# Two Silu paths of a fused Mamba and mixture kernel: tanh and a DVE product replaced by ACT's Silu

## What is computed

```
x_in = in_proj_w @ ctx;  xc = causal conv over 4 taps
u    = silu(xc + conv_b)                          # 512 channels x 512 steps
dt, B, C = x_proj_w @ u                           # the small projection, 16 + 16 + 16 rows
delta = softplus(dt_proj_w @ dt + dt_b);  A = -exp(A_log)
state[n] = state[n] * exp(delta * A[n]) + delta * u * B[n]      # scan over time, n = 0..15
y = sum_n state[n] * C[n] + D * u
x = x + tanh(g0) * y * silu(layernorm(x))         # z is layernorm(x), laid out channel by time
x = x + tanh(g1) * experts(layernorm(x))          # top 2 of 32, rank 16
```

## Time and profile before

| | us |
|---|---|
| median of 3 runs | 539.43 (539.42 to 541.25) |
| the profiled execution | 541.24 |
| its span | 539.4 |
| PE busy | 489.4 (91%) |
| DVE busy | 476.8 (88%) |
| POOL busy | 454.4 (84%) |
| ACT busy | 398.6 (74%) |

### The profile page before, as it was taken

The page is one execution under the profiler, slowest core; times in us unless marked ns, Lnnn a source line. Parts: engine busy times, 40 slices in busy tenths (PEclk is TensorE's granted clock), DMA queues, the critical chain, the costliest instruction groups (busy, mean ns, idle before and its releaser), DMA issues.

```text
span 539.4 us, 9244 instructions
## 1 busy us (share of the span) xinstructions
PE 489.4 (91%) x3018; PEld 367.8 (68%) x3018; DVE 476.8 (88%) x880; ACT 398.6 (74%) x726; POOL 454.4 (84%) x335
## 2 busy tenths in 40 slices
PE   9989798979677999999989999999899999899687
PEld 5569597758475776668677776667566666676654
DVE  3799999879899999789999999888988989999851
ACT  4698869386867777587968777577888898888542
POOL 1299999959999999979999999989799898987810
PEclk9979999999998999999998999999999999999799
...
DMA packets 18705, 39.36 MB, mean 73 GB/s; under 512 B 5586, under 2 KB 6354, under 8 KB 18659
## 3 DMA queue, kind: packets, MB, share of 16 engines
...
...
## 4 chain that ended last, share of the span: by engine, by line
PE 54%; DVE 19%; ACT 18%; issue 8%; DVEq 0%; POOL 0%; ACTq 0%; POOLq 0%
PE p_s L748 12%; PE p_y L770 11%; DVE state L1262 9%; PE p_v L803 8%; PE p_f L794 6%; ACT da L1007 4%; PE p_tr L717 4%; PE p_pr L692 2%; PE p_pr L680 2%; DVE p_s L1262 2%; ACT p_s L1007 2%; DVE x L1204 2%; ACT pair_b L991 2%; PE p_pr L673 2%; PE p_f L783 2%
## 5 line engine op out<-in xcount | busy, mean ns | idle before, releaser
L573 POOL TENSOR_TENSOR state<-state,c_bc 128x1024 f32<-128x1024 f32 (+1 forms) x131 | 256.7, 1973 | 21.5 <-DVE state L1262 19.2
L748 PEld LDWEIGHTS p_s<-pair_b,du_t 128*128 128x128 f32 x1072 | 139.2, 198 | 44.7 <-issue 31.4
L748 PE MATMUL p_s<-pair_b,du_t 128*128 128x128 f32 x1072 | 153.1, 285 | 16.7 <-DVE state L1262 13.8
L770 PE MATMUL p_y<-ident,state 128*128 128x128 f32 x1024 | 149.5, 276 | 0.0
L558 POOL TENSOR_TENSOR dbu<-du,pair_b 128x1024 f32<-128x1024 f32 (+1 forms) x80 | 145.3, 1818 | 1.7 <-DVE p_s L1262 1.7
L1007 ACT ACTIVATE p_s<-delta,a_neg 128x512 f32<-128x512 f32 (+1 forms) x162 | 93.5, 580 | 65.8 <-DVE state L1280 33.0
L1262 DVE TENSOR_TENSOR_SCAN state<-da,p_s 128x512 f32<-128x512 f32 (+1 forms) x116 | 134.4, 1173 | 6.3 <-PE p_s L748 5.7
L770 PEld LDWEIGHTS p_y<-ident,state 128*128 128x128 f32 x1024 | 121.6, 144 | 23.7 <-issue 22.7
L1007 ACT ACTIVATE da<-delta,a_neg 128x512 f32<-128x512 f32 (+1 forms) x158 | 100.4, 648 | 14.0 <-DVE state L1262 13.7
L1262 DVE TENSOR_TENSOR_SCAN state<-p_s,dbu 128x512 f32<-128x512 f32 (+1 forms) x100 | 98.2, 997 | 1.8 <-POOL dbu L558 1.8
L794 PE MATMUL p_f<-u_sb,h_t 128*128 128x512 f32 x112 | 55.9, 602 | 0.5 <-DVE gw L1365 0.5
...
## 6 DMA issues: line engine op xcount, KB each, us to landing
...
```

Of the source, the lines that this page charges most:

```text
L573: eng.tensor_tensor(pair, pair, c_bc[:, 2 * p:2 * p + 2, c0:c0 + w], ALU.mult).then_inc(po_cs, 1)
L748: mm = eng.matmul(p_s[g % BANKS][:, t * P:(t + 1) * P], du_t[:, f % 2, t, :], diagonals_of(n // 2)[:, n % 2, c0 // P + t, :], start=(t == ...
L770: mm = eng.matmul(p_y[:, t, :], slot(NS * f + n)[:, t * P:(t + 1) * P], ident[:, :], is_transpose=True, start=False, stop=(n == NS - 1 and ...
```

## The change

Both silus are computed by ACT's own function. The conv weights are not halved any more, `tanh_v`, `z_part` and DVE's two products go; `silu_u(q)` and `silu_z(f)` are one ACT instruction each, and the factor tanh(g0) goes into the copy of the turned gate (`copy_sz`). The Silu table is another set than that of Exp and Ln, so the silus are gathered in blocks `silu(f)`: a table load, one or two `silu_z`, none to two `silu_u`, and a load back. Exp and Ln are then both taken from one set, and the two loads around Ln go. The block stands at n = 9 behind decay 9 and the skip term, in phases 1, 3, 7 and 11 at n = 0 behind the first decay. There is a block in each of phases 1 to 12, and in 14, 16 and 18; phase 1 makes the gates of blocks 0 and 1 and u of block 5, phase 2 the gate of block 2 and u of blocks 4 and 6, phase f from 3 to 11 the gate of f and u of f + 4, and phases 12, 14, 16, 18 the gates of two halves. `zh` gets two buffers. The convolution of blocks 5 and up works in place in the ring of `u` and no longer in `vsp`; that ring has five slots in place of six. POOL's six small operations for z become four. PE and SP have the same instructions in the same order as before.

```diff
@@ -17,7 +17,7 @@
 BANKS = 3
-U_RING = 6
+U_RING = 5
...
@@ -134,6 +134,20 @@
+    SILU_Z = {1: [0, 1]}
+    SILU_Z.update({f: [f] for f in range(2, SPLIT)})
+    SILU_Z.update({f: [f, f + 1] for f in range(SPLIT, F, 2)})
+    SILU_U = {1: [5], 2: [4, 6]}
+    SILU_U.update({f: [f + 4] for f in range(3, SPLIT)})
+    def zh_before(f):
+        if f < SPLIT + 2:
+            return f - 2 if f < SPLIT else SPLIT - 2
+        return SPLIT - 1 if f < SPLIT + 4 else f - f % 2 - 3
     HELD = {11: [0, 1], 12: [2, 3], 13: [4, 5], 14: [6], 15: [7]}
...
@@ -188,8 +202,8 @@
         zv = sb("zv", [P, 2, Q])
-        zr = sb("zr", [P, 2, 4, Q])
-        zh = sb("zh", [P, L])
+        zr = sb("zr", [P, 2, 2, Q])
+        zh = sb("zh", [P, 2, L])
         sz_t = sb("sz_t", [P, Q, P])
...
@@ -356,7 +367,7 @@
-        ZOPS = 6
+        ZOPS = 4
         FOPS = 3
...
@@ -575,18 +585,14 @@
                 if b >= 2:
-                    eng.wait_ge(ac_z, 2 * Q * (b - 1))
+                    eng.wait_ge(ac_z, Q * (b - 1))
                 eng.tensor_tensor(zv[:, 0, :], zmv[:, :, 1], eps_c[:, :], ALU.add).then_inc(po_zs, 1)
                 eng.wait_ge(po_zs, ZOPS * b + 1)
-                eng.tensor_tensor(zv[:, 1, :], zv[:, 0, :], minus_half[:, :], ALU.pow).then_inc(po_zs, 1)
+                eng.tensor_tensor(zr[:, b % 2, 0, :], zv[:, 0, :], minus_half[:, :], ALU.pow).then_inc(po_zs, 1)
                 eng.wait_ge(po_zs, ZOPS * b + 2)
-                eng.tensor_tensor(zr[:, b % 2, 0, :], zv[:, 1, :], half[:, :], ALU.mult).then_inc(po_zs, 1)
-                eng.tensor_tensor(zv[:, 0, :], zv[:, 1, :], minus_half[:, :], ALU.mult).then_inc(po_zs, 1)
-                eng.wait_ge(po_zs, ZOPS * b + 4)
-                eng.tensor_tensor(zr[:, b % 2, 1, :], zmv[:, :, 0], zv[:, 0, :], ALU.mult).then_inc(po_zs, 1)
-                eng.wait_ge(po_zs, ZOPS * b + 5)
-                eng.wait_ge(ac_k, 2)
-                eng.tensor_scalar(zr[:, b % 2, 2:4, :], zr[:, b % 2, 0:2, :], gx[:, :], None, ALU.mult).then_inc(po_zs, 1)
+                eng.tensor_tensor(zv[:, 1, :], zmv[:, :, 0], zr[:, b % 2, 0, :], ALU.mult).then_inc(po_zs, 1)
+                eng.wait_ge(po_zs, ZOPS * b + 3)
+                eng.tensor_tensor(zr[:, b % 2, 1, :], zv[:, 1, :], minus_one[:, :], ALU.mult).then_inc(po_zs, 1)
...
@@ -919,18 +925,15 @@
                 eng.wait_ge(pe_in, q + 1)
-                if q >= 5:
-                    eng.wait_ge(ve_dl, q - 3)
+                if q >= U_RING:
+                    eng.wait_ge(ac_skip, q - U_RING + 1)
+                    wait_for_du(eng, q - U_RING)
                 eng.activation(conv_v(q), conv_bank(q)[:, :], ACT.Identity, bias=cb[:, q % Q:q % Q + 1],
-            def silu_first(q):
+            def silu_u(q):
                 eng.wait_ge(ve_tap, 3 * q + 3)
                 eng.activation(u[:, q % U_RING, :], conv_v(q), ACT.Silu).then_inc(ac_u, 1)
-            def tanh_v(q):
-                eng.wait_ge(ve_tap, 3 * q + 3)
-                eng.activation(conv_bank(q)[:, :], conv_v(q), ACT.Tanh).then_inc(ac_th, 1)
...
@@ -957,11 +960,12 @@
-            def copy_turn(kind, i, dest):
+            def copy_turn(kind, i, dest, scale=1.0):
                 eng.wait_ge(pe_turn, TURN[kind, i] + 1)
                 bank = turn_bank(kind, i)
-                eng.activation(dest, bank[:, :, 0:NS] if kind == "b" else bank[:, 0:blocks, :], ACT.Copy).then_inc(ac_turn, 1)
+                eng.activation(dest, bank[:, :, 0:NS] if kind == "b" else bank[:, 0:blocks, :], ACT.Copy,
+                               scale=scale).then_inc(ac_turn, 1)
...
@@ -1015,26 +1019,29 @@
-            def z_part(f, part):
+            def silu_z(f):
                 b, k, c0, w = PHASE[f]
-                source = xs[:, b % 2, k, c0:c0 + w]
-                if part == 0:
-                    eng.wait_ge(po_zs, ZOPS * (b + 1))
-                    eng.wait_ge(s_x[b % 2][k], 16 * (b // 2 + 1))
-                    if f:
-                        eng.wait_ge(pe_turn, TURN["sz", f - 1] + 1)
-                    eng.activation(zh[:, 0:w], source, ACT.Identity, bias=zr[:, b % 2, 3, k:k + 1],
-                                   scale=zr[:, b % 2, 2, k:k + 1]).then_inc(ac_z, 1)
-                else:
-                    if f >= 6:
-                        eng.wait_ge(ac_out, f - 5 if f < LAST else f - 6)
-                    eng.activation(p_v[:, 0:w], source, ACT.Tanh, bias=zr[:, b % 2, 1, k:k + 1],
-                                   scale=zr[:, b % 2, 0, k:k + 1]).then_inc(ac_z, 1)
+                eng.wait_ge(po_zs, ZOPS * (b + 1))
+                eng.wait_ge(s_x[b % 2][k], 16 * (b // 2 + 1))
+                if f >= 2:
+                    eng.wait_ge(pe_turn, TURN["sz", zh_before(f)] + 1)
+                eng.activation(zh_of(f), xs[:, b % 2, k, c0:c0 + w], ACT.Silu, bias=zr[:, b % 2, 1, k:k + 1],
+                               scale=zr[:, b % 2, 0, k:k + 1]).then_inc(ac_z, 1)
+            def silu(f):
+                eng.preload_act_table(ACT.Silu)
+                for i in SILU_Z[f]:
+                    silu_z(i)
+                for q in SILU_U.get(f, []):
+                    silu_u(q)
+                eng.preload_act_table_set("natural_log_exp_and_others")
                     eng.wait_ge(ve_x2, 2 * f)
-                copy_turn("sz", f, sz_t[:, 0:PHASE[f][3] // P, :])
+                eng.wait_ge(ac_k, 2)
+                copy_turn("sz", f, sz_t[:, 0:PHASE[f][3] // P, :], gx[:, :])
...
@@ -1162,17 +1171,11 @@
                         conv_first(f + 5)
-                    if n == 13:
-                        z_part(f, 0)
-                    if n == 14:
-                        z_part(f, 1)
-                        if f == 0:
-                            tanh_v(4)
+                    if n == 15 and f < LAST:
+                        copy_du(f + 1)
+                    if f in SILU_Z and n == (0 if f == 1 or turning else 9):
+                        silu(f)
                     if n == 15:
-                        if f < LAST:
-                            copy_du(f + 1)
-                        if f + 5 < BLOCKS:
-                            tanh_v(f + 5)
                         if Q <= f < EARLY + Q and f % Q:
...
@@ -1204,13 +1207,6 @@
                                          op0=ALU.mult, op1=ALU.add).then_inc(ve_tap, 1)
-            def silu_u(q):
-                eng.wait_ge(ac_th, q - Q + 1)
-                if q >= U_RING:
-                    eng.wait_ge(ac_skip, q - U_RING + 1)
-                eng.scalar_tensor_tensor(out=u[:, q % U_RING, :], in0=conv_bank(q)[:, :], scalar=1.0, in1=conv_v(q),
-                                         op0=ALU.add, op1=ALU.mult).then_inc(ve_u, 1)
...
@@ -1279,12 +1275,6 @@
-            def silu_z(f):
-                w = PHASE[f][3]
-                eng.wait_ge(ac_z, 2 * f + 2)
-                eng.scalar_tensor_tensor(out=zh[:, 0:w], in0=p_v[:, 0:w], scalar=1.0, in1=zh[:, 0:w], op0=ALU.add,
-                                         op1=ALU.mult).then_inc(ve_sz, 1)
             def gate_y(f, part):
...
@@ -1456,13 +1442,8 @@
                             f_statistics(T, 1)
-                        silu_z(f)
                         for T in stats[1:]:
                             f_statistics(T, 2)
-                    if f == 0 and n == 15:
-                        silu_u(4)
-                    if n == 15 and f + 5 < BLOCKS:
-                        silu_u(f + 5)
                     if (f, n) in c_by_dve:
...
```

More of the change, by code:

```diff
@@ L153, in flamingo @@
         minus_half = sb("minus_half", [P, Q])
-        half = sb("half", [P, Q])
+        minus_one = sb("minus_one", [P, Q])
         a_neg = sb("a_neg", [P, Q, NS])
@@ L298, in conv_v @@
         def conv_v(q):
-            return x2[:, q // Q, q % Q, :] if q < 5 else vsp[:, :]
+            return x2[:, q // Q, q % Q, :] if q < 5 else u[:, q % U_RING, :]
         def close_place(T, which):
@@ L380, in wait_for_du, with zh_of @@
                 eng.wait_ge(ve_du, 1)
-        def wait_for_u(eng, count):
-            if count <= Q:
-                eng.wait_ge(ac_u, count)
-            else:
-                eng.wait_ge(ve_u, count - Q)
+        def zh_of(f):
+            w = PHASE[f][3]
+            if f < SPLIT:
+                return zh[:, f % 2, :]
+            return zh[:, f // 2 % 2, w * (f % 2):w * (f % 2) + w]
         block = ctx.enter_context(nc.Block())
@@ L509, in _ @@
             eng.memset(minus_half[:, :], -0.5).then_inc(po_k, 1)
-            eng.memset(half[:, :], 0.5).then_inc(po_k, 1)
+            eng.memset(minus_one[:, :], -1.0).then_inc(po_k, 1)
             eng.iota(iota_i[:, :], [[1, S]], base=0, channel_multiplier=0).then_inc(po_k, 1)
```

45 lines of the change are left out of this document (20 added, 25 removed).

## The result

The changed kernel took **537.04 us** (median of 6 runs, 536.00 to 537.68), the kernel before 540.5 over all its runs beside it (539.42 to 541.41). The ratio is **0.9934**, 95% interval 0.9914 to 0.9954: 3.5 us faster. Forecast were 531.3 and 8.1 us. The sign and the range held, the size did not: less than half of the gain came, and 537.0 lies outside the forecast's own range. Of the 5.7 us between 531.3 and 537.0, 1.1 are the base: the forecast was taken from 539.43, the median of three runs, and over six runs the kernel before takes 540.5.

A forecast was written before the change was run, and what follows sets the result against it. No engine was taken to bound the whole; the chain passes through ACT, DVE and PE. Leads (how much earlier events come) summed along the phases to 8.1 us, taking the median from 539.43 to 531.3; range 526.5 to 540.0, own range 528.5 to 534.5.

The forecast's parts named there:

- what DVE has won it waits away: Phase 0 to 1: DVE loses three products but waits for decay 1 behind ACT's block; lead 0, bounds -0.5 to 1.
- Phase 1, predicted +0.3: Phase 1: DVE drops 1.16 us, but POOL has only 0.39 us idle; 0.3 taken of a possible 0 to 1.16.
- The tap's delay: Phase 2: ACT's block makes the convolution and so DVE's first tap 1.95 us late; bounds 1.3 to 2.5 of loss.
- the small projection: Phase 3: u of block 7 is ready 3.4 us later, against PE's earlier start at 4.4; 1.0 better.
- the Ln: Phases 3 and 4: its table load goes, so DVE's `delta` no longer waits 0.86 and 1.06 us for it.
- PE's wait for `h`: Phases 5 to 7: 1.09 us wait shrinks by 0.53 each, 1.6 together; phases 9 to 11: two times 0.53.
- DVE's 2.3 us a phase are nothing: Phases 5 to 7: PE is last, so DVE's 2.3 us a phase and a tap 0.4 late count nothing.
- a ring from which no instruction goes: Half phases: scan 6 waits for POOL, POOL for scan 11; only scan 9's 0.30 wait for PE can be won.
- A: Rival, chance 0.12: block waits not hidden, late taps count, PE waits at small projections of 3, 7, 11; 543.2 us, slower.
- B: Rival, chance 0.12: DVE is the bound, others only follow; some 13 us count after phase 2's wait, 526.4 us.
- C: Rival, chance 0.18: PE and POOL cover it; rest of phases 5 to 11 and halves give nothing; some 2.5 us, 536.9.
- D: Rival, chance 0.04: the skill page's drain comes with the blocks' explicit table loads; 6.5 us, giving 537.8 us.

The follow-up runs named there:

- PE kept busy: Changed kernel plus 14 matmuls of ones, never read, in phase 1 where PE waited 2.17 us for a scan; 536.77 us, ratio 0.9897.
- the run without loads: Changed kernel with gates 0 and 1 and u of block 5 by Identity and no table loads in phase 1; 533.23 us, ratio 0.9830.
- the run with ACT work before `h`: Changed kernel plus one whole-tile ACT operation ahead of `h` at the end of phases 5, 6, 7, 9, 10 and 11; 540.56 us, ratio 0.9988.
- the run with DVE work back: Changed kernel plus two unread whole-tile DVE statistics a phase, behind scans 0 and 15 of phases 5 to 10; 541.21 us, ratio 0.9997.

## Why the prediction was right and wrong

*The start, predicted 0, measured -1.5.* The step "what DVE has won it waits away" began at the end of phase 0. That POOL's four operations in place of six move its matrices was counted only in phase 4, as 0.5 of gain. The same move puts the matrices onto DVE's first products, an overlap that the prediction never looked at. All five runs in which the products meet no matrix, or only the end of one, have scan 0 earlier, by 1.0 to 1.6 us. This is the largest single miss.

*Phase 1, predicted +0.3, measured -0.6.* Block and wait were sized right (4.67 for 4.62; the products' 1.8 waited away), though the prediction's own sum had decay 1 end at 54.8 for a scan that began at 54.54 and booked nothing for it. Left out was what a wait of 2.1 us does to PE: it idles as long in its turn, and at half clock scan 7 waits 0.94 us. With PE kept busy the step is +0.3. That POOL held the phase was wrong, as the run without loads shows (0.9 gained in phase 1); the upper bound of 1.16 was nearer.

*Phases 2 and 3, predicted +1.1, measured +0.4.* The tap's delay took 2.1 of lead (predicted 1.95), the small projection gave 0.9 back (1.0), the Ln 1.0 (0.86), the products 1.2. Some 0.5 went in small waits that the sum had not, most of them before the tap. Phase 4 came as predicted step by step: the lead falls by 1.5 at scan 6, which waits for POOL (predicted 1.55), and regains 1.2 by the Ln (1.05).

*Phases 5 to 7, predicted +2.2 for DVE, measured +1.4.* PE's wait for `h` fell by 0.52 us in each of the five phases, as predicted (0.53), and the run with ACT work before `h` shows that it counts. But "DVE's 2.3 us a phase are nothing" is wrong: the run with DVE work back loses 0.6 for each statistic. The step that failed is the path: the sum followed PE alone, where DVE's own work is as much in it. In DVE's lead the products give 1.17 at the end of each phase, 3.5 in all. Against that stand 0.9 at scan 9 of phase 5, where the half clock comes on other work than before, 0.7 in phase 7, where scan 1 waits 2.52 us for the block and only 1.9 come back, and some 0.5 in small waits. The loads of phase 7 do not hide under PE's projection altogether. How much of the gain is PE's wait and how much DVE's products the two runs do not separate.

*Phases 9 to 11, predicted +1.7, measured +2.6.* 0.8 of this was no part of the sum. The kernel before had a half clock from 283 to 287 that is missing after; the first row is before, the second after:

```profile
282.00:288.00 6.00, 5.83 (x34) 5.40 (x34) 5.90 (x12) 3.58 (x7) 5.69 (x3) 0.72 0.01 3
...
282.00:288.00 6.00, 5.88 (x45) 4.99 (x46) 5.90 (x12) 3.67 (x7) 6.00 (x4) 1.00 0.02 4
```

*Half phases, predicted +2.2, measured +1.2 (0.4 of it behind the last scan).* I had called POOL and DVE a ring from which no instruction goes and still booked 0.3 a phase for scan 9's wait. The wait stayed at 0.30, and at scan 6 of phases 14 and 15 (and of 19) the product's 0.33 went to POOL.

*Rivals.* The place of A, the late tap, was real: moving the block gave 2.8 us, 0.9 of them in phase 5. Its price for PE in 7 and 11 was not paid: PE did not wait for u there. Of B it is true that DVE's products count at the ends of the phases, but not that the others only follow. C's number, 536.9, is the one measured, by luck: it takes the gains of phases 5 to 11 and of the halves for nothing, and they came (1.4, 2.6 and 1.2); what was lost was lost at the start and in phases 1 and 5. D falls: between decay and load lie 0.02 us, and each load takes 1283 ns. What the prediction had among no rival were the exclusion at the start and the clock.

Open is why the clock falls or not. In phase 5 the half clock lasts 3.5 us in one kernel and 7 in the next, though PE mostly idles 1.71 and 1.25 us ahead of it, and with 1.71 and 1.45 it stayed away in two runs. In phase 1 it fell behind 2.17 us of idle PE seven times and once not. The prices of the clock above are therefore those of single profiled runs.
